# A ten-block transformer kernel on one core: the last attention chain split, one batch projected inside the slots, the recurrent block reordered

## The reference, cut to what matters

```python
x = x + windowed_attention(ln(x))   # 16 heads of 8 channels, window +-16, token 0 global
x = x + ternary_ffn(ln(x))
x = x + recurrent(ln(x))
x = x + ternary_ffn(ln(x))
x = x + full_attention_1(ln(x))     # 16 heads, all 1024 x 1024 scores per head
x = x + experts(ln(x))              # route to the best of 8, at most 256 tokens each
x = x + full_attention_2(ln(x))
x = x + experts(ln(x))

def recurrent(x):                   # forward and backward direction d
    g = gelu(x)
    u = g @ Wx[d] + bx[d]
    a = sigmoid(u @ Wga[d] + bga[d]) * sigmoid(a_logit[d])
    i = sigmoid(u @ Wgx[d] + bgx[d]) * u * sqrt(1 - a * a)
    h[t] = a[t] * h[t-1] + i[t]     # a scan; backward in time for d = 1
    y = (sum over d of h @ Wo[d] + bo[d]) / 2 + x
    return gelu(y) @ ld_W + ld_b + x

def experts(x):
    p = softmax(x @ Wg); best = argmax(p); gate = max(p)
    place = running count of tokens sent to `best`
    return gate * (place < 256) * (x @ We + be)
```

## Time and profile before

| what | value |
|---|---|
| median of 3 executions | 1139.51 us (1138.41 to 1146.8) |
| the profiled execution: its own time | 1144.26 us |
| the profiled execution: its span | 1142.4 us |
| TensorE busy | 1001.0 us, 88% of the span |
| VectorE busy | 833.4 us, 73% |
| ScalarE busy | 752.0 us, 66% |
| GpSimd busy | 132.4 us, 12% |
| mean granted TensorE clock | 0.908 of full speed |

### The profile page before, as it was taken

One profiled execution on the slowest core, in us unless ns is written; L12 is line 12 of the kernel. 1 busy time (PEld: TensorE's weight loads), 2 busy tenths in 40 slices (PEclk: granted clock), 3 DMA queues, 4 the chain that ended last, 5 costly groups with the idle time before them and its releaser, 6 DMA issues.

```text
span 1142.4 us, 32326 instructions
## 1 busy us (share of the span) xinstructions
PE 1001.0 (88%) x13347; PEld 463.9 (41%) x13347; DVE 833.4 (73%) x1023; ACT 752.0 (66%) x1497; POOL 132.4 (12%) x416
## 2 busy tenths in 40 slices
PE   6799999782768999999899899999989999999964
PEld 2455455330333344444344344444434444344433
DVE  5446653536546999999779689978879997799412
ACT  3504446265431799998767689877779977699911
POOL 8100110000000000000102120010221001010000
PEclk8789999886877999999989899999999998899975
DMA  3753442100035132301000034200005410010000
GB/s 102 227 169 75 102 98 62 29 1 1 1 104 174 39 74 52 80 18 28 12 11 15 19 107 116 60 12 13 12 22 140 107 36 11 11 45 19 19 15 19
DMA packets 60386, 64.47 MB, mean 56 GB/s; under 512 B 17424, under 2 KB 39184, under 8 KB 60112
## 3 DMA queue, kind: packets, MB, share of 16 engines
q1 hardware_dynamic: 60240, 62.40, 20.6%
HBM read 27.06 MB, written 35.32 MB: 55 GB/s over the span
## 4 chain that ended last, share of the span: by engine, by line
DVE 48%; PE 38%; issue 5%; ACT 4%; DMA 3%; SPq 1%; POOL 0%; POOLq 0%; ACTq 0%; DVEq 0%
DVE nmf L1607 40%; PE wide L658 24%; PE bank L658 13%; DVE xcsq L1378 1%; DVE xp L1378 1%; ACT xcsq L1139 1%; DMA x<-xT 1%; ACT big L1139 1%; ACT L1139 1%; DVE xcsq L1387 1%; DVE big L1765 1%; ACT scr L1139 1%; SPq L433 1%; DMA KQs<-mw_dram 1%; DVE x L1378 1%
## 5 line engine op out<-in xcount | busy, mean ns | idle before, releaser
L1607 DVE TENSOR_REDUCE nmf<-wide 128x1 f32<-128x1024 f32 x512 | 591.0, 1221 | 50.5 <-PE wide L658 50.2
L1139 ACT ACTIVATE big<-wide 128x512 f32<-128x512 f32 x684 | 392.1, 602 | 92.9 <-PE wide L658 82.0
L658 PE MATMUL wide<-big,KQs 48*128 48x512 bf16 (+1 forms) x1376 | 358.8, 350 | 5.5 <-DVE nmf L1607 4.2
L658 PE MATMUL bank<-big,V 128*9 128x128 f32 x8192 | 328.8, 279 | 11.5
L658 PE MATMUL wide<-KQs,big 50*128 50x512 bf16 (+1 forms) x1036 | 273.2, 329 | 6.1 <-ACT big L1139 6.1
L658 PEld LDWEIGHTS bank<-big,V 128*9 128x9 f32 x8192 | 178.4, 91 | 239.4 <-ACT big L1139 194.2
L1139 ACT ACTIVATE big<-bank 128x512 f32<-128x512 f32 (+1 forms) x468 | 232.5, 515 | 45.2 <-PE bank L658 39.5
L658 PE MATMUL bank<-KQs,big 50*128 50x512 bf16 x340 | 133.0, 391 | 3.9 <-ACT big L1139 3.9
L1139 ACT ACTIVATE scr<-wide 128x380 f32<-128x380 f32 (+3 forms) x128 | 61.4, 487 | 84.2 <-PE wide L658 73.0
L658 PEld LDWEIGHTS wide<-KQs,big 50*128 50x128 bf16 x1036 | 70.3, 95 | 113.9 <-ACT big L1139 58.5
L1552 DVE TENSOR_REDUCE nmw<-wide 95x4 f32<-95x512 f32 (+1 forms) x96 | 60.7, 637 | 53.2 <-PE wide L658 52.3
(11 more groups left out here) (214 smaller groups left out, 813.1 us busy)
## 6 DMA issues: line engine op xcount, KB each, us to landing
o_dram<-big SPq DMA_DIRECT2D x128, 64.0 KB
big<-kf_dram SPq DMA_DIRECT2D x32, 200.0 KB
kf_dram<-scr SPq DMA_DIRECT2D x24, 256.0 KB, 3.3
qf_dram<-scr SPq DMA_DIRECT2D x24, 256.0 KB, 3.9
KQs<-qf_dram SPq DMA_DIRECT2D x32, 192.0 KB
ow_dram<-scr SPq DMA_DIRECT2D x32, 142.5 KB
big<-kw_dram SPq DMA_DIRECT2D x16, 275.0 KB
kw_dram<-scr SPq DMA_DIRECT2D x12, 352.0 KB, 5.6
```

Source lines behind the costliest of these rows:

```text
L658: return nc.tensor.matmul(o, l, r, start=start, stop=stop, **kw)
L1139: return nc.scalar.activation(o, i, f, **kw)
L1607: nc.vector.tensor_reduce(nmf[:, i % 4, c:c + 1], wide[:, k:k + 2, :].rearrange("p g c -> p (g c)"), AX.X, ALU.max, negate=True).then_inc( ...
```

## The change

- **Runs.** There are five: run 3 becomes chunk 2 alone, inside the slots from slot 115, and run 4 is chunk 3 alone after the last slot. In run 4 TensorE gets unused products ahead of most steps (`fill`), ScalarE squares and VectorE adds in GpSimd's place.
- **Expert block.** The one-hot choice is taken from the logits and not from the normalised probabilities; two operations of VectorE go, the exponential moves behind the choice, and the due times from `onehot` to `add` come 2 to 4 ticks earlier.
- **Projection.** `project_full` makes batch 0 only; batch 1 is projected by `project(p, name)` from tick 12 (slots 3 to 5), stored in slots 5 to 8 and loaded in slots 9 to 15.
- **First batch.** Heads 0 to 3 of each part are stored ahead of the others and loaded as soon as they are there. Keys go through SyncE's queue and queries through ScalarE's.
- **Order.** The means are spread after the projection, and `keep_busy(24)` becomes `keep_busy(18)` ahead of the waits.
- **Recurrent block.** The first product of each chunk is made inside the layer norm. GpSimd takes the eight squares, four of the eight multiplications by the root, and x + norm(x) for each chunk. Batch 0 goes first, and its scans start before batch 1's multiplications. The output products follow each scan with unused products between them; the bias goes into gelu, the halving into VectorE's addition, and the last two additions become one.

```diff
-RUNS = 4
+RUN_LAYER = (1, 1, 2, 2, 2)
+RUN_CHUNKS = ((0, 1), (2, 3), (0, 1), (2,), (3,))
-        START = tuple(4 * (ALL_SLOTS * (r + 1) // RUNS + (3 if r < 3 else 0)) for r in range(RUNS))
+        START = (4 * 35, 4 * 67, 4 * 99, 4 * 115, 4 * ALL_SLOTS)
+        PROJECTIONS = ((1, 1), (0, 2), (1, 2))
+        PSTART = (12, START[0] + 61, START[1] + 61)
+        FILL = {"sel": 26, "wo": 3, "mean1": 3, "var1": 6, "norm1": 4, "logits": 3, "gate": 8}
...
+        def first_batch(eng, k):
+            eng.wait_ge(fp_third, 2 * k + 2)
+            for j in range(6):
+                store_heads(eng, k, 0, j, 0, H // 4, part_first[k])
+            for j in range(6):
+                store_heads(eng, k, 0, j, H // 4, H, part_out[k])
+            eng.wait_ge(part_first[k], 96)
+            load_heads(eng, k, 0)
+            eng.wait_ge(part_out[k], 96)
+            load_heads(eng, k, 1)
...
# gpsimd
+            def recurrent():
+                pool.wait_ge(xn_ready, NC * 3)
+                for c in range(NC):
+                    pool.tensor_tensor(xch(x, c), xch(x, c), xn(c), ALU.add).then_inc(r_sum, 1)
+                for n in range(2 * NC):
+                    pool.wait_ge(r_decay, n + 1)
+                    a = rb[:, 1, 512 * n:512 * n + 512]
+                    pool.tensor_tensor(rc[:, 512 * n:512 * n + 512], a, a, ALU.mult).then_inc(r_square, 1)
+                for i, (d, c) in enumerate(ORDER):
+                    if c >= 2:
...
+                        pool.tensor_tensor(g, g, rc[:, 512 * n:512 * n + 512], ALU.mult).then_inc(r_drive, 1)
...
# tensor
+                keep_busy(18, bk(7))
+                pe.wait_ge(fp_res, 4)
+                pe.wait_ge(fp_v, 2)
...
-                keep_busy(24, bk(7))
...
+                pe.wait_ge(r_gate, 4 * NC)
+                keep_busy(24, bk(7))
+                outs(0, 0)
+                keep_busy(5, bk(7))
+                outs(1, 0)
+                keep_busy(4, bk(7))
+                outs(0, 1)
+                outs(1, 1)
...
# scalar
+                for d, c in ORDER:
+                    act.wait_ge(r_square, n + 1)
+                    fn(v, v, ACT.Sqrt, scale=-1.0, bias=ones[:, 0:1]).then_inc(r_root, 1)
...
                 if stage == 4:
-                    project_full(1)
+                    project_full()
+                    first_batch(act, 1)
                     full_attentions()
...
# vector
+                for i, (d, c) in enumerate(ORDER[0:NC]):
+                    dve.wait_ge(r_root, i + 1)
+                    tt(g, g, rc[:, at:at + 512], ALU.mult).then_inc(r_in, 1)
+                    if c == 1:
+                        dve.wait_ge(r_in, 2 * NC + i + 1)
+                        scan(d, 0)
                 for d in range(2):
+                    dve.wait_ge(r_drive, 2 * d + 2)
+                    scan(d, 1)
```

More of the change, by code:

```diff
@@ L312, in steps_at, with projections_at @@
                 for name in TICK:
+                    if name == "we1" and len(RUN_CHUNKS[r]) == 1:
+                        continue
                     if tick - START[r] == TICK[name] and (r < 2 or TICK[name] <= TICK["add"]):
                         yield r, name
+        def projections_at(tick):
+            for p in range(len(PROJECTIONS)):
+                for name in PTICK:
+                    if tick - PSTART[p] == PTICK[name]:
+                        yield p, name
         m_index, s_index = {}, {}
@@ L649, in _ @@
                             chain(r, name)
+                        for p, name in projections_at(tick):
+                            project(p, name)
             for tick in range(4 * (ALL_SLOTS - AHEAD + 1), END):
@@ L749, in project_window, with project_full @@
                     ins.then_inc(proj_mm, 1)
-            def project_full(layer):
+            def project_full():
                 done = []
-                for n, (kind, c, m) in enumerate(halves(layer)):
+                for n, (kind, c, m) in enumerate(FULL_CHUNKS):
                     if n >= CBUF:
@@ L980, in chain @@
                     if name == "sel":
[L981 to L982 removed]
+                        fill(r, FILL["sel"])
+                        for j, c in enumerate(chunks):
+                            blk = 4 * (layer - 1) + c
                             pe.wait_ge(o_rden, blk + 1)
[L984 to L985 removed]
+                            for g in range(4):
+                                ins = mm(wide[:, k + j, P * g:P * g + P], sel[:, g, :], rdenf[:, blk % 4, :])
@@ L986, in chain @@
                     if name == "wo":
+                        fill(r, FILL["wo"])
                         pe.wait_ge(mx_read, m_index[r, "sel"] + 1)
-                        for j in range(2):
-                            ins = mm(wide[:, k + j, :], w("wo%d" % layer), xch(aT, 2 * b + j))
+                        for j, c in enumerate(chunks):
+                            ins = mm(wide[:, k + j, :], w("wo%d" % layer), xch(aT, c))
                     if name in ("mean1", "mean2"):
                         if name == "mean1":
+                            fill(r, FILL["mean1"])
```

505 lines of the change are left out of this document (260 added, 245 removed).

## The result

The changed kernel takes 1135.09 us (median of 20 executions, 1125.94 to 1143.63), the kernel before 1140.78 us (20, 1133.06 to 1147.46). The ratio is 0.9949, with a 95% interval of 0.9929 to 0.9969: 5.8 us or half a per cent faster. The forecast was 28 us. Ratios leave out single executions more than 1.5% above the fastest of their kernel, among them one of 1493 us of oneq_fill; medians have all. The profiled execution has a span of 1133.2 us, 9.2 less than the 1142.4 before; mean granted clock 0.920 (0.908 before).

The account below looks back on a forecast made before the run. VectorE and TensorE were taken as alternating limits, nothing in a slot being free. Terms -26.5 + 19 + 6 - 12.6 - 12 - 1.5 = -27.6 took 1144.26 us to 1116.7 (median basis 1112); range 1101 to 1128.

Parts of the forecast that it names:

- the start of the slots: From projection to first maxima: first maximum at about 344 instead of 358.62 (-14.6), low clock +2, together -12.6 us.
- 348, behind all stores: Start of the slots: late bound, at 348 us, for the load landing behind all stores of both queues.
- Recurrent block: Recurrent block up to the next norm's root: earlier scans and fewer steps behind them, -12 us; -18 or -7 otherwise.
- The rival without it: Recurrent block: GpSimd does not hold up the scans, six us more gained, 1106 us; chance 0.15.
- Last run: Run behind the last slot, 54.5 us before: half the tokens, full clock and shorter steps save 26.5 us.
- the rival of a low clock: Last run: the clock stays low, -20 in place of -26.5 us, 1118 us; chance 0.15.
- Chunk 2's run in the slots: Slots around 115: a half run moved in costs +19 us where a full one costs 27.6; bounds 13.8 and 27.6.
- Batch 1's projection: Slots 3 to 5: the moved projection costs +6 us, between 5 and 9.
- slots at full price: Slots: a half run costs 27.6 us and the start gains 8, 1125 to 1128 us; chance 0.15.
- an in-order TensorE that stops VectorE: Slots: fourteen moved steps, each not ready on its tick, stop VectorE; at 4.6 us each 1152 us; chance 0.05.
- Three runs' shorter choice: Three runs inside the slots lose two small operations each, -1.5 us.

Follow-up runs that it names:

- oneq_fill: The changed kernel with all first-batch transfers on SyncE's queue and 72 unused products instead of 18 ahead of the first load: 1128.79 us, run again 1126.02 us.
- swap: The changed kernel with the two queues exchanged, keys on ScalarE's and queries on SyncE's: 1134.25 us, ratio to before 0.9974.
- oneq: The changed kernel with all first-batch transfers on SyncE's queue, the first load ahead of the other heads' queries: 1130.07 us, ratio to before 0.9943.
- unsplit: The changed kernel, still two queues, with blocks stored whole (12 stores instead of 24) and group 0's load behind them: 1130.5 us, ratio to before 0.9911.
- before_nofill24: The kernel before without its 24 unused products between the landed load and the first maximum: 1149.28 us, ratio to before 1.0081.
- One_end: The changed kernel with the last run's split undone, chunks 2 and 3 together behind the slots: 1128.41 us, ratio to before 0.9897.
- bridge: The changed kernel with 100 unused products instead of 18 ahead of the first load: 1122.74 us, ratio to before 0.9867.
- oneq_fill96: The changed kernel with all first-batch transfers on SyncE's queue and 96 unused products ahead of the first load: 1113.4 us, ratio to before 0.981.

## Why the prediction was wrong

**The failed step is the start of the slots**, forecast -12.6 us, measured +7.8: a miss of 20.4 us, where the sum (-27.6) and the balance (-9.2) lie 18.4 apart; the other misses nearly cancel. It has two halves.

- *The load, 9.3 us late.* Forecast was the first product 21.4 us behind the last norm tile's start (322.56 to 344); measured 30.7. I took 0.63 us an issue from a row with one queue at work for a stretch with two. The stores took 1.23 us on ScalarE's queue, so the query load went out 23.7 us behind the norm tile instead of 16.4; it landed 7 us later instead of 4 to 5. The bound "348, behind all stores" (25.4) was too near as well. swap showed that SyncE's queue can be as slow (1.24), oneq that one queue, sorted, is 4.0 us faster, unsplit that two queues with half the stores are 3.1 us faster. What makes the issue slow is open: the engine, the order of start and the pair of queues were not separated. I had weighed the Trainium skill, DMA: Bandwidth & Descriptors, section "Issuing engines are not separate DMA queues", as a gain of 2.5 us by the issue alone. By this trace not even the issue gained, and the measurement decides: 24 stores took 16.8 us on two queues and 17.0 on one. Nor did I ask whether the rate survives smaller stores. Whole blocks moved 324 GB/s on one queue (336 to 343 us of the kernel before) and 321 on two (unsplit); split ones moved 202 to 220 on two queues (320 to 332 us), with the DMA engines 0.72 to 0.76 busy and so not full.
- *The clock, 11.1 us.* From first product to first score 17.8 us before, 30.9 after, +13.1 where I had +2. I saw that TensorE would wait and that the clock had been low in such a gap, but let it stay low for 5 us. It lasted until 376, through all sixteen maxima and into the first slot. The 0.66 that I read in the earlier trace rows is a mean of 0.50 up to 356 us and 0.96 and more behind it, and what stands at the step is the 24 unused products. I took them for dead time behind a landed load; the change drops them, and they are what raised the clock there (before_nofill24). No part of my list priced what the change removes at this place.

**Recurrent block:** -12 forecast, -14.4 measured. The cause was right: GpSimd and VectorE hold each other up, and scans count. The Trainium skill, SBUF — State Buffer, section "Who interferes with whom", gave this; the trace agrees, with 3.24 and 3.28 us for the scans beside GpSimd and 2.2 for those without. The rival without it fell. The sizes in it were less right than the total: 4.8 us were won ahead of the last scan's end, where 1.7 were forecast, because the first multiplication came 1 us sooner and the hold-up was 4 us and not 6; the 9.6 behind it stand against 10.1.

**Last run:** -26.5 forecast, -27.9 measured, by the steps that were listed. Clock 1.00; the rival of a low clock fell.

**Chunk 2's run in the slots:** +19 forecast; from 1028.89 to 1088.09 stand 36 maxima, 59.2 us less 36 x 1.14, +18.2. **Batch 1's projection:** +6 forecast; 21 maxima from 376.18 to 408.13, 31.95 less 23.9, make +8.0. The rivals with slots at full price or an in-order TensorE that stops VectorE fell: a half run costs 18.2 us of the 27.6 of a full one.

**Three runs' shorter choice:** 49 maxima pass from 930 to 1010, but the 46 of the earlier trace rows are those from 926 to 1006; from 930 to 1010 the kernel before has 48, so this shows next to nothing; over all slots what is left besides the two terms above is -0.4, with an estimated 3 us for the low clock in the first slot in it (four maxima from 369 to 376 us, 7.2 us where 4.6 are usual). The -1.5 is not contradicted, and not shown.

**What the sum hid.** Every term but one was right to 2.4 us, and yet the sum could not say that its largest pair was a loss. I set -26.5 against +19 as if the one paid for the other. One_end shows that 15.5 of it came free of the split. The split by itself saves 12.4 and costs some 18, and is a loss of 5 to 6 us, which is what the ratios say too (0.9949 and 0.9897, 5.9 us).

## What to carry to other kernels

Price each part of a bundled change against the kernel that has all other parts, not against the kernel before; a part can ride on its neighbours' gain. Where filler keeps TensorE warm, follow it up to the first product that matters: it has to end behind the event that it bridges, and 2.5 us short was nearly as bad as 18 (starts of 56.6 and 57.6 us). Before a second DMA queue is opened, look at the busy share of the DMA engines in that stretch and at how many issues it takes, not at the issue time of a queue that was alone; and put the load that is waited for ahead of the stores that it does not need (oneq did this together with the single queue; by itself it was not tried).

## What the runs showed of the hardware

- **The clock and the density of work.** From 340 to 360 us of the changed kernel TensorE is busy for nearly the whole time by the (modelled) records and the clock stays at 0.50; it rises at 376, when score and value products have begun to fill the slots. In the run with 72 unused products a gap of 2.46 us behind 15.7 us of dense products was enough for it to fall: the first product behind the gap took 0.59 us, and the window from 336 has 0.50; gaps of 0.2 to 0.7 us in the last run were not, nor was one of 0.73 us behind 21.5 us of products (bridge, the traced execution). I expected it to come back by itself in 5 us.
- **A low clock need not cost.** Without the fillers the same maxima ran at 1.19 us at 1.2 GHz, against 1.14. It cost 0.79 us each only with two unused products between them.
- **Issue on two queues.** A store took 0.62 to 0.82 us on one queue. With both at work it took 0.81 on SyncE's and 1.23 on ScalarE's as changed, 0.82 and 1.17 in unsplit, and with the tensors exchanged 1.24 and 1.12. The queue with the queries, the second to be ready, was the slower each time, and ScalarE's never took under 1.12. What makes it so was not tried further.
- **Split stores.** In these windows it is the split and not the number of queues that goes with the lower rate: whole blocks moved 324 GB/s on one queue and 321 on two, blocks split at a quarter of the heads 202 to 220 on two queues and 218 to 243 on one (oneq_fill96 and oneq, 324 to 328 us).
- **A scan and GpSimd hold each other up too.** GpSimd's four multiplications took 2.19 us on average, the one beside two scans 3.24, where an addition of the same size took 1.26; two scans paid 1.0 us each, and the one with GpSimd idle nothing.
